# Attention with the values' product swapped, query heads turned whole, and an order of steps for each engine

## The chip, the core and the metric

The kernel runs on one core of a Trainium2 chip. The metric is the device time in microseconds (us) of one execution. The core has five engines with a queue each: TensorE (PE; its weight loads are shown apart as PEld), VectorE (DVE), ScalarE (ACT), GpSimd (POOL) and SyncE (SP), which here issues DMAs. They meet by semaphores only. SBUF is the working memory with 128 partitions, PSUM the banks that TensorE writes (8 banks of 128 partitions x 512 f32), DRAM the memory outside.

## What is computed

The input x is 8 sequences of 512 tokens with 256 channels. The reference adds to it a block "conditioning attention, then delta rule mixer", and then two mixtures of experts. Only the attention is touched here. Reduced to what matters:

```
q = norm(x) @ Wq            # 16 heads of 64
k, v = norm(x) @ Wkv        # one head of 64, shared by all query heads
s = 8 * l2norm(q) . l2norm(k) + relative bias, causal over key chunks, plus one null key
p = softmax(s)
o = p @ v   (null key: + p_null * v_null)
h = layernorm(o @ Wout)     # goes on to the delta phase, channels turned onto partitions
```

## The kernel before

Three phases follow one another: attention (`attention_phase`), the delta rule (`delta_phase`) and the mixtures. Between phases all engines meet.

**Tiles and heads.** The attention works on 32 query tiles of 128 tokens (`t`, 8 batches x 4). Tile i of a batch looks at i+1 key chunks of 128 keys; this number of chunks is w (1 to 4), and `width(n)` is 128 w. Each tile has 16 heads, numbered through as n = 16 t + h, 512 in all. One head is: scores (L455, two products of a 128-row operand that holds the high and the low part of the query, 64 rows each, with kT high and kT low); on VectorE the bias is added and the row minimum taken (L697); on ScalarE the exponential and its sum (L874); w transposes on TensorE (L465); their eviction from PSUM to PT, by VectorE for every fourth head (L708), else by ScalarE (L883); and the values' product (L478), for each key chunk one 128x128 f32 stationary operand PT with v as 64 moving columns. Its result stands with queries on partitions in the banks OB, 8 heads each. An f32 product is two records of the profile, a transpose or a product of fp32r is one. TensorE works with lags: in step n it does scores of head n, transposes of head n-2 (`QK_LAG`), the values' product of head n-4 (`PV_LAG`). GpSimd makes bias plus mask (L968) some heads ahead.

**Side steps.** Between the heads, each tile needs steps of its own. In front of its heads (`FRONT`, slots given against the tile before): statistics of x (stat, on DVE and POOL), xn, its turn xT, the projections q0, q1 and kv (L544), the sums of squares ss (POOL raises them to -0.5, L1001), qn, the turn of k (kT, L751 to L754), null, then the split of qn into high and low parts side by side in qs (qs0, qs1: cast on ACT L916, subtraction on POOL L1022), and the turns qT0 to qT3, four transposes each (L556), two copied out by ACT (L920) and two by DVE (L740). Behind its heads (`BACK`): diff and weigh per half of the heads, where the denominators become reciprocals rden and the null key's weights pnr, and the 8 heads of a bank are scaled into o (L616); oT, eight transposes (L569), copied out by ACT (L934) and DVE (L773); pnT, the turn of pnr (L575, L778); outp, the product with Wout plus the null key's part (L582, L583); statistics of the result, hn (L790), hT (L588, L940), and SP's store of it (L412).

**Order and banks.** `order()` merges heads and side steps into one list, which every engine walks; each does its own part of a step, in this order, and nothing overtakes. The side steps that need a PSUM bank share two, F0 and F1, as `FILLS` says. `fill` makes TensorE wait until the previous holder of the bank has been read, `filled` makes the reader wait for TensorE.

Of the kernel before, what the change touches and what calls it, by code (L numbers as in the profile page):

```python
# [6 lines left out]
F32 = mybir.dt.float32  # L7
# [5 lines left out]
P = 128  # L13
# [130 lines left out]
def attention_phase(nc, a, ident, delta, mixture, hT_out, bias_rows, hT_dram, inv_dram):  # L144


    QK_LAG, PV_LAG, S_SLOTS, PT_SLOTS = 2, 4, 5, 3
# [3 lines left out]
    with ExitStack() as ctx:  # L151
# [37 lines left out]
        qs = sb("qs", [P, NH, 2, DH], F32R)  # L189
# [7 lines left out]
        with ExitStack() as over:  # L197
            def mlp(name, shape):
# [26 lines left out]
        rden = sb("rden", [P, 2, NH // 2])  # L225
        pnr = sb("pnr", [P, P])
        pnrT = sb("pnrT", [P, P])
        o = sb("o", [P, NH, DH])
        stats2 = sb("stats2", [P, 6])
# [27 lines left out]
                 "q_high", "q_low", "kn_ready", "qT_act", "qT_dve", "kT_read", "kT_ready", "null_ready",  # L257
                 "scores_psum", "scores_ready", "probs_ready", "probsT_psum", "probsT_act", "probsT_dve", "pv_done",
                 "null_diff", "null_probs", "weights_ready", "o_scaled", "oT_act", "oT_dve", "pnrT_ready",
# [8 lines left out]
        mask_loaded = [sem(f"mask_loaded{i}") for i in range(2)]  # L268


        FRONT = {"stat": -5, "xn": -3, "xT": -2, "q0": 0, "q1": 1, "kv": 2, "ss": 3, "qn": 4, "kT": 7,
                 "null": 10, "qs0": 8, "qs1": 9, "qT0": 12, "qT1": 12, "qT2": 13, "qT3": 14}
        BACK = {"diff1": 0, "weigh1": 4, "oT": 6, "pnT": 7, "outp": 9, "hn": 11, "hT": 13}

        def order():
            behind = {}
            for t in range(NT + 1):
                if t < NT:
                    behind.setdefault(NH * t + 10, []).append(("diff0", t))
                    behind.setdefault(NH * t + 13, []).append(("weigh0", t))  # L280
                if t > 0:
                    for n, h in BACK.items():
                        behind.setdefault(NH * t + h, []).append((n, t - 1))
            for t in range(1, NT):
                for n, h in FRONT.items():
                    behind.setdefault(max(NH * (t - 1) + h, -1), []).append((n, t))
            behind.setdefault(6, []).append(("nullo", 0))
            for h in range(NH):
# [4 lines left out]
                     ("qs0", 0), ("qs1", 0), ("qT0", 0), ("qT1", 0), ("qT2", 0), ("qT3", 0),  # L293
                     ("narrow", 0)] + behind.get(-1, [])
            for n in range(NH * (NT + 1)):
                steps += [("head", n)] * (n < NH * NT + PV_LAG) + behind.get(n, [])
            return steps

        steps = order()
# [4 lines left out]
        for name, t in steps:  # L304
            for n in ([0, 1] if name == "oT" else [FILLS[name]] if name in FILLS else []):
                filling[name, t, n] = len(held[n]) + 1
                before[name, t, n] = held[n][-1] if held[n] else None
                held[n].append((name, t))

        def drained(name, t, n):  # L310
# [3 lines left out]
                    "qT0": [(s["qT_act"], 2 * t + 1)], "qT1": [(s["qT_dve"], 2 * t + 1)],  # L314
                    "qT2": [(s["qT_act"], 2 * t + 2)], "qT3": [(s["qT_dve"], 2 * t + 2)],
                    "kT": [(s["kT_read"], t + 1)], "oT": [((s["oT_act"], s["oT_dve"])[n], t + 1)],
# [3 lines left out]

        def evac_by_dve(n):
            return n % 4 == 3

        def count_dve(n):

            return (n + 1) // 4
# [28 lines left out]
        with nc.Block() as block:  # L355
            @block.sync
            def _(sp):
# [26 lines left out]
                for name, t in steps:  # L384
# [20 lines left out]
                    elif name == "head" and t % (NH * TT) == 0 and t // (NH * TT) + 2 < B:  # L405
                        b = t // (NH * TT)
                        sp.wait_ge(s["mask_read"], b + 1)
                        load_mask(b + 2)
# [13 lines left out]
            def _(pe):  # L422
# [16 lines left out]
                for name, t in steps:  # L439
                    if name == "head":  # L440
# [28 lines left out]
                        if 0 <= n < NH * NT:  # L469
# [5 lines left out]
                            if h == 8 and tile > 0:  # L475
                                pe.wait_ge(s["o_scaled"], 2 * tile)
# [2237 lines left out]
```

## Time and profile before

| | |
|---|---|
| time, median of 3 runs | 2559.46 us (2557.53 to 2559.73) |
| span of the profiled execution | 2563.2 us, mean granted clock 0.984 |
| first scores / last values' product of the attention | 55.0 / 1083.3 us |
| start of the delta phase | about 1099.6 us |
| TensorE busy | 2394.0 us, 93% of the span |
| VectorE / ScalarE / GpSimd busy | 1753.9 / 1234.0 / 1333.1 us |

The profile is one execution. No time of it is given beside the span; the span is 3.7 us above the median of the runs. A record of TensorE lasts from its start to its modelled end, and records overlap, so that the sum of durations is no time; what tells the pace is the distance of starts or of ends. Busy time counts overlapping records once.

### The profile page before, as it was taken

The page shows a single profiled execution, that of the slowest core. Times are in us where ns is not written, and L with a number is a line of the kernel's source. Part 1 is how long each engine was busy: PE and PEld are TensorE (multiplying, and loading weights), DVE is VectorE, ACT ScalarE, POOL GpSimd, SP SyncE. Part 2 cuts the span into 40 slices and gives each one's busy share as a digit, 9 for nine tenths or more (in the row PEclk, how much of TensorE's full clock was granted, in tenths as well). Part 3 has the DMA queues.
Part 4 walks back from the last instruction along what each step waited for, and adds up shares of the span by engine and source line. Part 5 has one row for each costly group of instructions (what it writes and reads, how often), then busy time and mean ns, then how long its engine had stood idle before and what let it go on. Part 6 is the DMA issues. An engine that isn't in the chain of part 4 may idle for free. (4 is left out here: it accounts for less than half of the span.)

```text
span 2563.2 us, 56453 instructions
## 1 busy us (share of the span) xinstructions
PE 2394.0 (93%) x20705; PEld 1977.5 (77%) x20705; DVE 1753.9 (68%) x4121; ACT 1234.0 (48%) x3133; POOL 1333.1 (52%) x1464
## 2 busy tenths in 40 slices
PE   5999999999999999977999999988899999999998
PEld 3788888888888888845777777766677877778776
DVE  4576767677767676677888888337865755746764
ACT  3656666666666666554555555114333333332332
POOL 3676767676767676535666666215422322322332
PEclk8999999999999999988999999999999999999999
DMA  4000100000000000001122221216022112111211
GB/s 143 7 11 9 46 18 11 10 10 9 11 10 9 10 5 5 5 15 24 40 56 55 55 53 47 55 59 181 32 66 63 55 58 67 58 47 62 66 34 59
DMA packets 156689, 105.05 MB, mean 41 GB/s; under 512 B 85168, under 2 KB 134832, under 8 KB 156416
## 3 DMA queue, kind: packets, MB, share of 16 engines
q1 hardware_dynamic: 130928, 62.69, 9.0%
q10 hardware_dynamic: 25488, 38.73, 4.9%
q8 instruction: 169, 2.77, 0.4%
q14 instruction: 104, 0.85, 0.1%
HBM read 80.51 MB, written 20.88 MB: 40 GB/s over the span
## 5 line engine op out<-in xcount | busy, mean ns | idle before, releaser
L968 POOL TENSOR_TENSOR a_bm<-a_bias,a_mask_add 128x512 f32<-128x512 f32 (+3 forms) x512 | 438.4, 873 | 189.3 <-DVE a_nm L697 186.3
L1592 POOL TENSOR_TENSOR m_hid_part<-m_hid,m_hid_part 128x512 fp32r<-128x512 f32 x176 | 238.5, 1355 | 552.9 <-ACT m_hid_part L1501 547.6
L874 ACT ACTIVATE a_S<-a_S,a_nm 128x512 f32<-128x512 f32 (+3 forms) x512 | 289.3, 565 | 347.6 <-DVE a_nm L697 344.9
L697 DVE CUSTOM_DVE_ANT_0 a_S<-a_S,a_bm,a_nsn 128x512 f32<-128x512 f32 (+3 forms) x512 | 275.3, 545 | 142.1 <-PE a_S L455 137.4
L478 PE MATMUL a_O<-a_v,a_PT 128*128 128x64 f32 x2560 | 342.4, 265 | 0.0
L478 PEld LDWEIGHTS a_O<-a_v,a_PT 128*128 128x128 f32 x2560 | 328.4, 193 | 0.0
L1513 ACT ACTIVATE m_hid<-m_G 128x512 f32<-128x512 f32 x176 | 105.4, 599 | 390.9 <-PE m_G L1447 353.3
L455 PE MATMUL a_S<-a_kT,a_qT 128*128 128x384 f32 (+3 forms) x1024 | 284.0, 358 | 3.6 <-DVE a_nm L697 3.2
L1674 DVE TENSOR_TENSOR m_hid<-m_hid,m_U 128x512 f32<-128x512 f32 x176 | 121.0, 687 | 223.8 <-PE m_U L1447 190.3
L1464 PE MATMUL m_Y<-m_hid_part,m_down_high 128*128 128x512 f32 x704 | 256.5, 405 | 12.2 <-POOL m_hid_part L1592 11.4
L1447 PE MATMUL m_G<-m_in,m_gate_high 128*128 128x512 f32 x704 | 252.2, 399 | 0.9 <-POOL m_up_low L1586 0.9
L1447 PE MATMUL m_U<-m_in,m_up_high 128*128 128x512 f32 x704 | 250.7, 396 | 1.5 <-DVE m_hid L1674 1.4
L465 PE MATMUL a_T<-s_ident,a_S 128*128 128x128 f32 x1280 | 227.0, 275 | 12.2 <-ACT a_PT L883 11.3
L465 PEld LDWEIGHTS a_T<-s_ident,a_S 128*128 128x128 f32 x1280 | 160.3, 140 | 42.2 <-ACT a_S L874 15.7
L455 PEld LDWEIGHTS a_S<-a_kT,a_qT 128*128 128x128 f32 x1024 | 163.8, 192 | 18.5 <-DVE a_nm L697 6.6
L1464 PEld LDWEIGHTS m_Y<-m_hid_part,m_down_high 128*128 128x128 f32 x704 | 132.8, 189 | 47.4 <-issue 18.0
L1447 PEld LDWEIGHTS m_U<-m_in,m_up_high 128*128 128x128 f32 x704 | 132.7, 188 | 35.0 <-DVE m_hid L1674 3.0
L1447 PEld LDWEIGHTS m_G<-m_in,m_gate_high 128*128 128x128 f32 x704 | 133.3, 189 | 33.9 <-POOL m_up_low L1586 1.4
L883 ACT COPY a_PT<-a_T 128x128 f32<-128x128 f32 (+3 forms) x384 | 156.2, 407 | 0.0
L1447 PE MATMUL m_G<-m_in,m_gate_low 128*128 128x512 f32 x352 | 140.6, 399 | 0.0
L1001 POOL TENSOR_TENSOR a_rr<-a_ss,a_half 128x17 f32<-128x17 f32 x32 | 98.5, 3077 | 79.8 <-DVE a_ss L736 79.8
L1464 PE MATMUL m_Y<-m_hid_part,m_down_low 128*128 128x512 f32 x352 | 139.4, 396 | 0.0
(323 smaller groups left out, 5348.4 us busy)
## 6 DMA issues: line engine op xcount, KB each, us to landing
m_spread<-s_w ACTq DMA_DIRECT2D x64, 256.0 KB, 3.2
m_spread<-s_w ACTq DMA_DIRECT2D x128, 128.0 KB, 2.9
a_x<-in_x SPq DMA_DIRECT2D x32, 128.0 KB, 2.2
s_hT<-a_hT SPq DMA_DIRECT2D x32, 128.0 KB, 2.1
d_x<-in_x SPq DMA_DIRECT2D x8, 512.0 KB, 4.7
d_h<-s_hT SPq DMA_DIRECT2D x8, 512.0 KB, 5.2
s_xg<-d_xg SPq DMA_DIRECT2D x8, 512.0 KB, 3.1
d_x<-s_xg SPq DMA_DIRECT2D x8, 512.0 KB, 4.6
```

What stands on the lines that cost most here:

```text
L455: last = pe.matmul(o_s[:, 0:w], qT[:, tile % 2, h], kT[tile // TT % 2][i][:, 0:w], start=i == 0, stop=i == 1)
L465: last = pe.transpose(TB[n % 2][:, j * P:(j + 1) * P], S[:, n % S_SLOTS, j * P:(j + 1) * P], ident[:])
L478: last = pe.matmul(OB[h // 8][:, (h % 8) * DH:(h % 8 + 1) * DH], PT[:, n % PT_SLOTS, j * P:(j + 1) * P], v[tile // TT % 2][:, j], start=j ...
L697: dve.tensor_tensor_reduce(S[:, n % S_SLOTS, 0:w], SB[n % 2][:, 0:w], bm[:, n % BM_SLOTS, 0:w], -1.0, nsn[:, tile % 2, h:h + 1], ALU.add, ...
L874: act.activation(S[:, n % S_SLOTS, 0:w], S[:, n % S_SLOTS, 0:w], ACT.Exp, scale=-1.0, bias=nm[:, tile % 2, h:h + 1], accum_out=den[:, tile ...
L883: act.copy(PT[:, n % PT_SLOTS, 0:w], TB[n % 2][:, 0:w]).then_inc(s["probsT_act"], 1)
L968: pool.tensor_tensor(bm[:, n % BM_SLOTS, 0:w], bias[:, h, L - w:L], mask_add[b % 2][:, 0:w], ALU.add).then_inc(s["bm_ready"], 1)
L1447: last = pe.matmul(dst[q % 2][:, :], wts[m][j][:, k, item], x[i][:, k], start=(i, j, k) == TERMS[0], stop=(i, j, k) == TERMS[-1])
L1464: last = pe.matmul(YB[k][:, :], down[m][j][:, item, k * P:(k + 1) * P], hid_part[i][:, q % H_SLOTS], start=item == 0 and i + j == 0, stop= ...
L1513: act.activation(hid[:, q % G_SLOTS], GB[q % 2][:, :], (ACT.Copy, ACT.Silu)[ITEMS[q][1]]).then_inc(gate_active, 1)
L1592: pool.tensor_tensor(hid_part[1][:, q % H_SLOTS], hid[:, q % G_SLOTS], hid_part[0][:, q % H_SLOTS].bitcast(F32), ALU.subtract).then_inc(hi ...
L1674: dve.tensor_tensor(h, h, UB[q % 2][:, :], ALU.mult).then_inc(mult_up, 1)
```

## The change

- The values' product works on two heads at once, after the second (odd) one. v is now the stationary operand, 128 rows by 64 columns, PT the moving one with 128 columns. The even head's result goes to partitions 0 to 63 of the bank, the odd one's to 64 to 127. So it comes out turned, channels on partitions, as the product with Wout wants it: the oT transposes and their copies go. PT has four slots instead of three.
- The reciprocals of the denominators stood one per partition and now must stand along the free axis, the same for 64 partitions. They are turned on TensorE (first half: new step wT0, 128x8; second half: in eight rows of pnT), copied to SBUF by VectorE, written to DRAM by SyncE and, once landed, read back to 64 partitions each with a zero stride, two transfers per half, 128 KB each. New steps scale0 and scale1 multiply the banks with them straight into oT.
- qn is turned whole, two heads per transpose, 8 per tile; the split follows. ScalarE copies one half of the partitions as the high part to its place, VectorE subtracts and writes the low part to the other half. qs and its two steps on ScalarE and GpSimd go.
- VectorE evicts one head of 16 (head 13) instead of four.
- One table SLOTS with offsets for each engine (LATER) takes the place of FRONT and BACK; each engine walks its own order. The banks F0 and F1 are dealt anew. The step outp is split into outp (TensorE) and ostat (statistics).

```diff
-    QK_LAG, PV_LAG, S_SLOTS, PT_SLOTS = 2, 4, 5, 3
+    QK_LAG, PV_LAG, S_SLOTS, PT_SLOTS = 2, 4, 5, 4
...
+        LATE = slice(2 * NH, 2 * NH + NH // 2)
+        weight = o[:].rearrange("p (i a) d -> p i (a d)", i=2)
...
+        SLOTS = {"stat": -21, "xn": -19, "xT": -18, "q0": -15, "q1": -15, "kv": -14, "ss": -13, "qn": -11, "kT": -9,
+                 "null": -7, "qT0": -8, "qT1": -7, "diff0": 7, "weigh0": 9, "wT0": 12, "diff1": 16, "scale0": 15,
+                 "weigh1": 14, "pnT": 19, "scale1": 24, "outp": 25, "ostat": 27, "hn": 28, "hT": 32}
+        LATER = {"PE": {}, "DVE": {"weigh1": 3, "ostat": -2, "scale0": 3, "weigh0": -1, "xT": 1, "pnT": 1, "qT1": 1,
+                 "diff1": -1, "hn": 1}, "ACT": {"hT": -1, "qT0": -1, "diff1": -1}, "POOL": {"qn": -1, "ostat": -1,
+                 "ss": 1}, "SP": {}}
...
+                behind.setdefault(max(NH * t + h + LATER[engine].get(n, 0), -1), []).append((n, t))
...
-        FILLS = {"xT": 0, "q0": 1, "q1": 0, "kv": 1, "qT0": 0, "qT1": 1, "qT2": 0, "qT3": 1, "kT": 0,
-                 "pnT": 1, "outp": 0, "hT": 1, "nullo": 0, "wide0": 0, "wide1": 1}
+        FILLS = {"xT": 1, "q0": 1, "q1": 0, "kv": 1, "qT0": 0, "qT1": 0, "kT": 0, "pnT": 0, "outp": 1, "hT": 0, "wT0":
+                 0, "nullo": 0, "wide0": 0, "wide1": 1}
...
+        DVE_HEADS = {13}
...
 sync:
+                    elif name in ("wT0", "pnT"):
+                        i = int(name == "pnT")
+                        sp.wait_ge(s["pnrT_ready" if i else "weightT_ready"], t + 1)
+                        sp.dma_start(weight_rows[i], pnrT[LATE, :] if i else weightT[:]).then_inc(weight_out, 16)
+                        sp.wait_ge(weight_out, 16 * (2 * t + 1 + i))
...
+                            sp.wait_ge(s["o_scaled"], 2 * t - 1 + i)
+                        for e in range(2):
+                            sp.dma_start(weight[e * DH:(e + 1) * DH, i].rearrange("p (a n) -> p a n", n=P),
+                                         bass.AP(tensor=weight_rows.tensor, offset=(i * NH // 2 + e) * P,
+                                                 ap=[[0, DH], [2 * P, NH // 4], [1, P]])).then_inc(weight_in[i], 16)
 tensor, head:
-                        if 0 <= n < NH * NT:
+                        if 0 <= n < NH * NT and n % 2 == 1:
...
-                                last = pe.matmul(OB[h // 8][:, (h % 8) * DH:(h % 8 + 1) * DH],
-                                                 PT[:, n % PT_SLOTS, j * P:(j + 1) * P], v[tile // TT % 2][:, j],
-                                                 start=j == 0, stop=j == tile % TT)
+                                for e in range(2):
+                                    last = pe.matmul(OB[h // 8][e * DH:(e + 1) * DH, at:at + P], v[tile // TT % 2][:, j],
+                                                     PT[:, (n - 1 + e) % PT_SLOTS, j * P:(j + 1) * P],
+                                                     start=j == 0, stop=j == tile % TT, skip_group_check=True)
...
-                            last = pe.transpose(f[:, j * P:(j + 1) * P],
-                                                qs[:, 4 * i + j].rearrange("p a d -> p (a d)").bitcast(F32), ident[:])
+                            last = pe.transpose(f[:, j * P:(j + 1) * P],
+                                                qn[:, 8 * i + 2 * j:8 * i + 2 * j + 2].rearrange("p a d -> p (a d)"), ident[:])
...
+                    elif name == "wT0":
+                        pe.transpose(f[0:NH // 2, 0:P], rden[:, 0], ident[:]).then_inc(full[FILLS[name]], 1)
 vector:
+                    to = pnr[:, LATE] if i else rden[:, 0]
+                    dve.reciprocal(to, dent[:, i]).then_inc(s["rden_ready"], 1)
...
+                def scale(t, i):
+                    dve.wait_ge(weight_in[i], 32 * (t + 1))
+                    dve.wait_ge(s["pv_done"], NH // 2 * t + 4 * (i + 1))
...
+                    dve.tensor_tensor(oT[:, 4 * i:4 * i + 4].rearrange("p a n -> p (a n)"), OB[i][:, :], weight[:, i],
+                                      ALU.mult).then_inc(s["o_scaled"], 1)
...
+                            dve.wait_ge(s["qT_high"], 4 * t + 2 * i + e + 1)
+                            dve.tensor_tensor(turned_heads(t, i, e)[other], heads_of(f)[own],
+                                              turned_heads(t, i, e)[own].bitcast(F32),
+                                              ALU.subtract).then_inc(s["qT_low"], 1)
 scalar:
-                        act.copy(qs[:, hs, 0], qn[:, hs]).then_inc(s["q_high"], 1)
+                        for e in range(2):
+                            act.copy(turned_heads(t, i, e)[halves(e)], heads_of(f)[halves(e)]).then_inc(s["qT_high"], 1)
 gpsimd:
-                        pool.tensor_tensor(qs[:, hs, 1], qn[:, hs], qs[:, hs, 0].bitcast(F32),
-                                           ALU.subtract).then_inc(s["q_low"], 1)
```

## Rows read from the trace of the kernel before

**Rows 1.** The page: busy time by engine, and the chain that ended last

```profile
PE 2394.0 (93%) x20705; PEld 1977.5 (77%) x20705; DVE 1753.9 (68%) x4121; ACT 1234.0 (48%) x3133; POOL 1333.1 (52%) x1464
...
PE 26%; DVE 2%; issue 2%; POOL 1%; ACT 0%; DMA 0%; ACTq 0%; SPq 0%; POOLq 0%; DVEq 0%
```

**Rows 2.** Busy time by stretch, four tiles of the third batch (w = 1, 2, 3, 4)

```profile
318.80:345.60 26.80, 24.30 (x178) 21.89 (x177) 16.65 (x65) 16.05 (x62) 17.13 (x24) 1.00 0.02 6
345.60:373.80 28.20, 25.77 (x185) 23.13 (x184) 20.93 (x66) 17.68 (x63) 21.41 (x25) 1.00 0.10 31
373.80:407.50 33.70, 31.75 (x236) 29.39 (x234) 25.35 (x66) 21.06 (x64) 26.19 (x25) 1.00 0.04 12
407.50:446.10 38.60, 38.34 (x283) 34.88 (x282) 27.82 (x68) 24.19 (x64) 26.01 (x26) 1.00 0.03 9
```

**Rows 3.** Groups by line and form, attention, TensorE: busy us, mean ns, idle before

```profile
L478 PE MATMUL a_O<-a_v,a_PT 128*128 128x64 f32 x2560 | 342.4, 265 | 0.0
```

**Rows 4.** Timeline of TensorE: start, length, records; w = 4, then the last heads

```profile
701.33 0.60 PE L465 MATMUL a_T<-s_ident,a_S 128*128 128x128 f32 x4
701.77 1.00 PE L478 MATMUL a_O<-a_v,a_PT 128*128 128x64 f32 x8
702.58 0.42 PE L455 MATMUL a_S<-a_kT,a_qT 128*128 128x128 f32 x2
...
1080.49 2.79 PE L478 MATMUL a_O<-a_v,a_PT 128*128 128x64 f32 x24
```

**Rows 5.** Timeline in the delta phase, then L2182 by record: min/median/max in ns

```profile
1299.67 0.41 PE L2235 MATMUL d_O<-d_S,d_qpT 64*32 64x64 f32 x8
1300.01 1.09 PE L2182 MATMUL d_R<-d_attn,d_uw 128*64 128x128 f32 x16
1301.04 0.44 PE L2092 MATMUL d_R<-s_ident,d_y 128*128 128x128 f32 x2
...
L2182 PEld LDWEIGHTS d_R<-d_attn,d_uw x256: 132/137/137, 1220.0 to 1685.9; 128*64 128x64 f32 x128
L2182 PE MATMUL d_R<-d_attn,d_uw x256: 272/273/323, 1220.0 to 1686.0; 128*64 128x128 f32 x128
```

**Rows 6.** Waits of TensorE, 60 to 1150 us: total us, times, longest

```profile
PE a_F L556 <- DVE a_hn L790: 11.6, 16, 0.9
...
PE a_F L556 <- ACT a_qT L920: 7.8, 24, 0.6
...
PE a_F L588 <- DVE a_qT L740: 5.2, 9, 1.0
PE a_F L575 <- DVE a_oT L773: 3.7, 8, 0.9
```

**Rows 7.** Groups by line and form on ACT, DVE and POOL, 60 to 1150 us

```profile
L883 ACT COPY a_PT<-a_T 128x512 f32<-128x512 f32 x96 | 54.2, 565 | 0.0
L916 ACT CAST a_qs<-a_qn 128x512 fp32r<-128x512 f32 x62 | 37.9, 611 | 0.0
L883 ACT COPY a_PT<-a_T 128x128 f32<-128x128 f32 x96 | 23.8, 247 | 0.0
...
L740 DVE CAST a_qT<-a_F 128x512 fp32r<-128x512 f32 x62 | 42.5, 685 | 8.8 <-PE a_F L556 8.7
L773 DVE COPY a_oT<-a_F 128x512 f32<-128x512 f32 x32 | 22.1, 691 | 24.1 <-PE a_F L569 24.1
...
L1022 POOL TENSOR_TENSOR a_qs<-a_qn,a_qs 128x512 fp32r<-128x512 f32 x62 | 78.9, 1272 | 3.8 <-ACT a_qs L916 3.8
```

**Rows 8.** DMA issues: KB each, median us to landing; page, then 60 to 1100 us

```profile
m_spread<-s_w ACTq DMA_DIRECT2D x128, 128.0 KB, 2.9
...
a_mask_in<-in_mask SPq DMA_DIRECT2D x5, 64.0 KB, 3.2
...
d_chunk_of<-in_c_chunk_of SPq DMA_DIRECT2D x1, 2.0 KB, 1.7
```

**Rows 9.** Timeline of TensorE at the end of the attention, in brackets idle time before

```profile
1086.92 5.33 PE L582 MATMUL a_F<-a_wout,a_oT 128*128 128x256 f32 x16 [0.59 <-DVE a_pnrT L778]
```

More of the change, by code:

```diff
@@ L188, in attention_phase @@
         kn = sb("kn", [P, 2, DH])
-        qs = sb("qs", [P, NH, 2, DH], F32R)
         qT = sb("qT", [P, 2, NH, P], F32R)
@@ L268, in attention_phase, with order @@
         mask_loaded = [sem(f"mask_loaded{i}") for i in range(2)]
[L271 to L275, printed above, removed]
-            behind = {}
[L277 to L286, printed above, removed]
+        weight_out = sem("weight_out")
+        weight_in = [sem(f"weight{i}_in") for i in range(2)]
+        SLOTS = {"stat": -21, "xn": -19, "xT": -18, "q0": -15, "q1": -15, "kv": -14, "ss": -13, "qn": -11, "kT": -9,
[4 more added lines that the diff above has]
+                 "ss": 1}, "SP": {}}
+        BACK = ("diff0", "weigh0", "wT0", "diff1", "scale0", "weigh1", "pnT", "scale1", "outp", "ostat", "hn", "hT")
+        def order(engine):
+            behind = {}
+            for t in range(NT):
+                for n, h in SLOTS.items():
+                    if t > 0 or n in BACK:
+                        behind.setdefault(max(NH * t + h + LATER[engine].get(n, 0), -1), []).append((n, t))
             behind.setdefault(6, []).append(("nullo", 0))
@@ L383, in _ @@
                 sp.dma_start(inv_dram.rearrange("s t h c i j -> (s t h c) (i j)"), null_flat).then_inc(s["inv_cleared"], 16)
-                for name, t in steps:
+                for name, t in order("SP"):
                     if name == "layer" and t == 1:
@@ L437, in fill @@
                     return FB[n]
-                for name, t in steps:
+                for name, t in order("PE"):
                     if name == "head":
@@ L546, in _ @@
                         last.then_inc(full[FILLS[name]], 1)
-                    elif name in ("qT0", "qT1", "qT2", "qT3"):
+                    elif name in ("qT0", "qT1"):
                         i = int(name[2])
@@ L768, in _ @@
                         weigh(t, int(name[5]))
-                    elif name == "oT":
-                        f = filled("oT", t, 1)
-                        if t > 0:
-                            dve.wait_ge(full[0], filling["outp", t - 1, 0])
-                        dve.tensor_copy(oT[:, 4:8].rearrange("p a n -> p (a n)"), f[:, :]).then_inc(s["oT_dve"], 1)
+                    elif name == "wT0":
+                        f = filled(name, t)
+                        dve.tensor_copy(weightT[:], f[0:NH // 2, 0:P]).then_inc(s["weightT_ready"], 1)
+                    elif name in ("scale0", "scale1"):
+                        scale(t, int(name[5]))
                     elif name == "pnT":
@@ L823, in _ @@
                                   a["L0_cond_Wkv"][k * P:(k + 1) * P, :]).then_inc(w_loaded[k], 16)
-                for name, t in steps:
+                for name, t in order("ACT"):
                     if name == "gain":
@@ L929, in _ @@
                         act.activation(pn[:, i], dn[:, i], ACT.Exp).then_inc(s["null_probs"], 1)
-                    elif name == "oT":
-                        f = filled("oT", t, 0)
-                        if t > 0:
-                            act.wait_ge(full[0], filling["outp", t - 1, 0])
-                        act.copy(oT[:, 0:4].rearrange("p a n -> p (a n)"), f[:, :]).then_inc(s["oT_act"], 1)
                     elif name == "hT":
@@ L974, in _ @@
                 link(pool.memset(pnr[:], 0.0))
-                for name, t in steps:
+                for name, t in order("POOL"):
                     if name == "head":
@@ L1003, in _ @@
                         pool.wait_ge(s["rr_ready"], t + 1)
+                        if t > 0:
+                            pool.wait_ge(full[FILLS["qT1"]], filling["qT1", t - 1])
                         pool.wait_ge(s["q_ready"], 2 * (t + 1))
```

163 lines of the change are left out of this document (75 added, 88 removed).

## The prediction, made before the changed kernel ran

> **What bounds the kernel now.** I first read the page for the engine shares and the slices. TensorE is busy 2394.0 of 2563.2 us; the chain that ended last reaches back only into the mixtures, 26% of the span on TensorE and 2% on the next [rows 1]. The attention, which alone is changed, ends at 1096 us, its heads run from 55 to 1083. So the second view is the busy time by stretch over one batch of four query tiles, one of eight alike [rows 2]. The reader is to see that TensorE idles 0.26 us in the widest tile (38.34 of 38.60), 1.95 in the next, 2.4 and 2.5 in the two narrow ones. VectorE has 10.8, 8.3, 7.3 and 10.1 us left in them, ScalarE more. So TensorE's own work is the bound in the wide tiles, and in the narrow ones a chain of small waits between engines. Third come the groups of TensorE: the values' product (L478) is the costliest, 342.4 us [rows 3]. Fourth, its timeline, since a mean of pipelined records doesn't tell their pace. Last, the waits [rows 6], for what the new order can remove.
>
> **Values' product: from 128x64 moving to two 64-column tiles.** In the widest tile the transposes end at 701.33+0.60 = 701.93, the 8 records of one head at 701.77+1.00 = 702.77, and the next scores at 703.00 [rows 4]. So 8 records take 0.84 us from end to end, near 0.112 each, the first 0.06 (24 in a row take 2.79 us [rows 4], 0.109 each without the last one's latency). With w key chunks a head takes 0.17, 0.40, 0.62, 0.84 us for w = 1 to 4, and a pair of heads twice that.
> After, a pair of heads has 4w records again, but two by two in the column halves of the array. No row of the attention shows that. The delta phase has the same form, 128 rows x 64 columns with 128 moving, alternating halves as here: 16 records in 1.09 us [rows 5]; less one record's latency of 0.273, 15 steps of 0.054, so two records per 0.109. The price is a change of the array's shape at both sides. Into that form: the records before end at 1300.08, the 16 at 1301.10, 1.02 us where 8 steps of 0.109 are 0.87, so 0.15 extra. Out of it: two transposes end 0.38 us later where 0.22 is usual, so 0.16 extra. A pair of heads then takes 0.218w + 0.31 = 0.53, 0.75, 0.96, 1.18 us, against 0.34, 0.80, 1.24, 1.68: +0.19, -0.05, -0.28, -0.50. There are 8 batches x 8 pairs of each width: 64 x (-0.64) = **-41 us**. Bounds: the switches can't cost less than nothing (-120), and at 0.45 us instead of 0.31 the sum is -5. I take the measured 0.31, as that form is the same.
>
> **Transposes.** A full 128x128 one costs 0.11 us ((0.60-0.27)/3 [rows 4]). The turn of query heads whole takes 8 instead of 16 of them per tile, and the 8 of the output go (L569). One small one (128x8) is new. 32 x (16 x 0.109 - 0.11) = **-52 us**. Together -93: -10 in a tile with four chunks, hardly anything in one with a single chunk beyond the transposes' 1.6.
>
> **The other engines.** ScalarE loses two casts of 0.611 and the 512-wide copy to oT per tile, gains two 512-wide copies (four half-height ones for two full ones) and 3 of 16 more evictions, 0.247 to 0.565 each: +0.1 to +1.1 us. VectorE loses two casts of 0.685, the copy of 0.691 and three evictions, at most as long, gains four subtractions of half height from PSUM (I take 0.69, as the 512-wide cast from PSUM; 0.35 if height counts, 1.0 if the crossing of halves does) and the small copy of the turned weights, under 0.3: +0.1 to -1.1. The scaling stays one product per half. GpSimd loses two of 1.272 [rows 7]. All this fits beside TensorE: in the widest tile VectorE would have 26.7 us of 32 to do, ScalarE 25.3. What is close is not the sum but where they block.
>
> **Waits that go.** The new turn stands on a bank whose holder before was kT, not outp; oT, which filled both banks, is gone. The four waits that hang on this are 11.6, 7.8, 5.2 and 3.7 us [rows 6]: **-28 us** (0 to -40, the latter as small waits hide in the latency of records that count as busy).
>
> **Waits that come.** (1) qT1 fills the bank that qT0 filled one head before; it is free after two copies on ScalarE and two subtractions on VectorE, some 0.59+3x0.69 = 2.7 us after the transposes, while one head of a narrow tile lasts under 1.2 us on TensorE. (2) The reciprocals now travel: turned, written to DRAM, read back to 64 partitions each by two transfers, all on SyncE. A small transfer lands in 1.7 us; a broadcast of 64 KB took 3.2, one of 128 KB 2.9 [rows 8]. With 0.6 us for the issue between: 1.7+0.6+3.2 = 5.5 to 6. For the first half this lies between slots 12 and 18 and is hidden. For the second, VectorE copies pnrT at slot 20 and waits in scale1 at slot 24 of the next tile, four heads: some 2.7, 4.2, 5 and over 6 us by that tile's width (an estimate: per head 0.34 us of scores and one transpose at w = 1 [rows 4], a pair of products every second head, and above that ScalarE, which has some 0.7 to 1.2 us for each head). So it is late by 3, 1.5, 0.8 and 0. Behind scale1 stand VectorE's next heads and its subtractions for qT0, thus qT1 and outp on TensorE; two heads of slack absorb a part, and (1) falls together with it. I take 5.5 us per batch for both: **+44 us**. Bounds: 0 if the trip takes 4 us and ScalarE has its copies done; at 8 us it is 5.3+3.8+3+2 = 14 per batch, 112.
> SyncE's queue holds x loads, masks and hT's store beside these; at the points passed none waits for anything later than the transfers do, so nothing there is added.
>
> **The two ends.** At the end nothing hides the trip: before, the last product ends at 1083.3 and outp starts at 1086.92 [rows 9]. After, pnT no longer waits for the product, its trip of 5.5 to 6 us starts near 1082.5 on that scale, then 0.7 for the scaling: outp at 1089.5, **+3**. In front of the first head qT1's wait for the bank costs 2.7 us and the two split steps that go give back 0.6 + 1.3 [rows 7]: **+1**.
>
> **Sum.** -93 - 28 + 44 + 4 = -73 us. The profiled execution has a span of 2563.2, 3.7 above the median 2559.46 of the runs; in runs: **2486 us**.
>
> **A rule against this.** The record rows say loads run beside the matmuls in flight: 16 loads of up to 0.137 us lie within the 1.09 us of the 16 records [rows 5]. The Trainium skill, page "TensorE: Matmul & The Clock Gate", section "Part 3: Packing small matmuls — row/col tiling", says that a weight load overlaps with matmuls in flight only where the row group differs, and two column halves share their rows. By that rule, each of the 1280 record pairs would show its load; as a mechanism of this kernel that is 1280 x 0.137 = +175 us, 2661 in all. The trace disagrees with it at the same form.
>
> **Rivals.**
> A. *The new waits are hidden.* The trip takes near 4 us or the lead of two heads takes it up. Then -93-28+4, 2442 us. For: VectorE has 7 to 10 us left per tile [rows 2]. Against: those are exactly the narrow tiles where TensorE already waits though nobody is full.
> B. *The trip is long.* 8 us, as SyncE's two broadcasts have small pieces (512 bytes) and come one behind the other: -93-28+112+4 = -5, so 2554; about 2545 where slack absorbs some. For: broadcasts are the slowest small transfers of rows 8. Against: the queues are near empty in the attention, a DMA share of 0.02 to 0.10 [rows 2].
> C. *The halves don't run side by side*, since here each record adds to the sum of the one before last in the same bank. Then a pair of heads costs 0.218w more, mean 0.545, x 256 = +140: 2626, **slower than before**. Place: L478's successor; it decides from where about half of the overlap is lost. It is also the case in which the change doesn't do what it says. Against: 0.054 per record in rows 5, though there every product stands alone.
> D. The exposed loads above, 2661.
>
> **Chances.** My forecast 0.46, A 0.25, B 0.22, C 0.05, D 0.02. Beside the forecast's own 2465 to 2507, the range goes 2430 to 2542: it leaves out C and D, about 0.1 of B and little of A. A measurement of this kernel tells 0.2% (5 us) from no change; faster by more: 0.46 + 0.25 + most of B = 0.90; within: 0.02; slower: 0.08 (C, D and the end of B).
>
> **What would show it.** The product's group has 2560 records of 128*64 with 128 moving, two starting within a few ns, and its busy time falls to 200 us or less; a pair of heads ends 1.18 us behind its transposes at w = 4 and 0.53 at w = 1 (wrong: 2.0 and 0.75, rival C). The widest tile lasts 33 us instead of 38.6, the narrowest stays near 26. Waits: TensorE's on qT's low half and VectorE's on the weights' DMA, longest behind slot 24 in the narrow tiles; if the DMA's is under 1 us, A; over 3 in wide tiles too, B. From the last product to outp some 6 us instead of 3.6. All behind the attention keeps its length; if it doesn't, the forecast is wrong for a reason not named here.

## The result, and the profile after

The changed kernel takes 2532.3 us (median of 4 runs, 2526.3 to 2541.4), the kernel before 2559.6 on the same chip. The ratio is 0.9889, 95% interval 0.9859 to 0.9918: 27 us faster. The forecast was 73 us faster. Direction and range held, the size was less than half of the forecast.

The page of the changed kernel (busy time, share of the span, instructions; the granted TensorE clock in 40 slices of the span; then two groups of its list), beside [rows 1, 3]:

```profile
PE 2324.1 (92%) x20225; PEld 1800.3 (71%) x20225; DVE 1751.1 (69%) x4089; ACT 1257.3 (50%) x3197; POOL 1259.7 (50%) x1400
...
PEclk8998989899999999898999999999999999999999
...
L492 PE MATMUL a_T<-s_ident,a_S 128*128 128x128 f32 x1280 | 234.7, 281 | 35.7 <-ACT a_PT L914 32.8
L508 PE MATMUL a_O<-a_PT,a_v 128*64 128x128 f32 x2560 | 202.8, 289 | 0.4 <-ACT a_PT L914 0.4
```

The values' product falls from 342.4 to 202.8 us, as forecast (200 or less). TensorE as a whole loses only 69.9 us of busy time, where 93 us of work went. The clock's row has 8s among the first ten slices; the same row of the kernel before is

```profile
PEclk8999999999999999988999999999999999999999
```

The busy time by stretch, the third batch again, tiles with one to four key chunks, beside [rows 2] (length, then busy time of TensorE, of its weight loads, of VectorE, ScalarE, GpSimd; granted clock, DMA share, GB/s):

```profile
308.30:337.70 29.40, 26.11 (x163) 20.10 (x161) 17.97 (x67) 16.71 (x66) 14.47 (x21) 0.83 0.07 21
337.70:366.00 28.30, 25.31 (x171) 19.30 (x169) 19.78 (x65) 18.11 (x64) 18.18 (x22) 0.94 0.16 47
366.00:396.10 30.10, 28.35 (x222) 22.55 (x218) 24.30 (x67) 21.83 (x66) 23.78 (x23) 1.00 0.12 34
396.10:431.10 35.00, 33.19 (x267) 26.21 (x265) 28.04 (x67) 25.33 (x66) 24.98 (x26) 1.00 0.10 30
```

Before, these four took 26.8, 28.2, 33.7 and 38.6 us, all at a clock of 1.00. The wide tiles gained 3.6 us each. The narrowest got 2.6 us longer, and its TensorE is busy 1.8 us more, though it has less to do: its clock is 0.83.

Where that comes from stands in the timeline of TensorE in that tile (start, length, records; in brackets the idle time before and what ended it):

```profile
317.19 0.44 PE L508 MATMUL a_O<-a_PT,a_v 128*64 128x128 f32 x4
317.78 0.44 PE L482 MATMUL a_S<-a_kT,a_qT 128*128 128x128 f32 x2
318.55 0.30 PE L492 MATMUL a_T<-s_ident,a_S 128*128 128x128 f32 x1 [0.33 <-ACT a_PT L914]
...
321.08 0.47 PE L590 MATMUL a_F<-s_ident,a_kn 128*128 128x128 f32 x1 [1.32 <-POOL a_kn L1028]
321.21 0.67 PE L482 MATMUL a_S<-a_kT,a_qT 128*128 128x128 f32 x2
...
323.68 0.70 PE L508 MATMUL a_O<-a_PT,a_v 128*64 128x128 f32 x4
324.52 5.27 PE L604 MATMUL a_F<-a_wout,a_oT 128*128 128x256 f32 x16
...
330.42 0.42 PE L482 MATMUL a_S<-a_kT,a_qT 128*128 128x128 f32 x2
```

The same four records of the product take 0.44 us at 317.19 and 0.70 at 323.68; the same two of the scores 0.44, 0.67, and 0.42 again from 330.42. In between the clock records show half of the full 2.4 GHz, that is 1.2. Before it fell TensorE had had single transposes and pairs of records between short waits, last one of 1.32 us. Summed over the 31 tiles behind the first, TensorE is at the lower level (1.2 GHz) for 88.8 us; before, for none.

The waits of TensorE from 60 to 1080 us (total, times, longest), beside [rows 6]:

```profile
PE a_T L492 <- ACT a_PT L914: 32.8, 75, 0.7
PE a_F L604 <- DVE a_oT L645: 24.6, 24, 6.0
PE a_F L590 <- POOL a_kn L1028: 9.2, 7, 1.3
...
PE a_F L558 <- DVE a_xn L748: 4.8, 6, 1.0
...
PE a_F L610 <- DVE a_hn L822: 2.1, 1, 2.1
```

The four waits that were to go are gone. The 2.1 us on hn stand at the very end, as they do in the trace of before; new are 2.1 us of query heads' turns on GpSimd's qn and 1.2 us of wT0 on qT. In the trace of before, from 60 to 1080 us, the wait of a transpose for ScalarE's copy was

```profile
PE a_T L465 <- ACT a_PT L883: 11.3, 30, 0.5
```

and is 32.8 now; outp's for the scaled output (24.6, of which 6.0 at the very end) and kT's for kn are new or larger.

**The ledger.** From the records of both profiled runs, TensorE, in us, what changed against before:

| part | forecast | measured |
|---|---|---|
| tiles 2 to 32, TensorE busy (930.4 to 867.5) | -93 | -62.9 |
| tiles 2 to 32, TensorE idle (56.6 to 80.5) | -28 + 44 = +16 | +23.9 |
| first tile (35.6 to 38.3) | +1 | +2.7 |
| last scores to the delta phase (21.9 to 25.1) | +3 | +3.2 |
| in front of the first head, and all behind the attention | 0 | +0.3 - 5.9 |
| span (2563.2 to 2524.5) | -73 | -38.7 |

The profiled run of the changed kernel is the fastest of its four, hence 38.7 here and 27 in the medians. A second profile of it has the same middle (948.7 us for tiles 2 to 32 against 948.0) and a span of 2534.1; of the 9.6 us between the two spans 7.2 lie behind the attention, which the change doesn't touch, and 2.7 in the first tile. The row to explain is the first: 30 us of busy time.

### The profile page after: what moved, and what is told of

It is laid out like the page before. It is cut to its first block and busy times, and to the rows that moved or that the text cites. A ratio compares the mean times of both kernels' runs of the same rounds, so it can differ in the third digit from the quotient of the medians.

```text
span 2524.5 us, 55790 instructions
## 1 busy us (share of the span) xinstructions
PE 2324.1 (92%) x20225; PEld 1800.3 (71%) x20225; DVE 1751.1 (69%) x4089; ACT 1257.3 (50%) x3197; POOL 1259.7 (50%) x1400
## 5 line engine op out<-in xcount | busy, mean ns | idle before, releaser
L482 PE MATMUL a_S<-a_kT,a_qT 128*128 128x384 f32 (+3 forms) x1024 | 294.4, 372 | 4.5 <-DVE a_nm L725 1.9
L1475 PE MATMUL m_Y<-m_hid_part,m_down_high 128*128 128x512 f32 x704 | 256.5, 405 | 12.3 <-POOL m_hid_part L1603 11.5
L492 PE MATMUL a_T<-s_ident,a_S 128*128 128x128 f32 x1280 | 234.7, 281 | 35.7 <-ACT a_PT L914 32.8
L508 PE MATMUL a_O<-a_PT,a_v 128*64 128x128 f32 x2560 | 202.8, 289 | 0.4 <-ACT a_PT L914 0.4
L482 PEld LDWEIGHTS a_S<-a_kT,a_qT 128*128 128x128 f32 x1024 | 170.3, 204 | 42.7 <-DVE a_nm L725 20.5
L914 ACT COPY a_PT<-a_T 128x128 f32<-128x128 f32 (+3 forms) x480 | 198.8, 414 | 1.4
L508 PEld LDWEIGHTS a_O<-a_PT,a_v 128*64 128x64 f32 x2560 | 137.0, 139 | 43.3 <-issue 36.3
L604 PE MATMUL a_F<-a_wout,a_oT 128*128 128x256 f32 x512 | 131.8, 415 | 25.3 <-DVE a_oT L645 24.6
```

What stands on the lines that cost most here:

```text
L482: last = pe.matmul(o_s[:, 0:w], qT[:, tile % 2, h], kT[tile // TT % 2][i][:, 0:w], start=i == 0, stop=i == 1)
L492: last = pe.transpose(TB[n % 2][:, j * P:(j + 1) * P], S[:, n % S_SLOTS, j * P:(j + 1) * P], ident[:])
L508: last = pe.matmul(OB[h // 8][e * DH:(e + 1) * DH, at:at + P], v[tile // TT % 2][:, j], PT[:, (n - 1 + e) % PT_SLOTS, j * P:(j + 1) * P], ...
L604: pe.matmul(f[:, 0:D], oT[:, i], wout[:, i], start=i == 0, stop=False)
L914: act.copy(PT[:, n % PT_SLOTS, 0:w], TB[n % 2][:, 0:w]).then_inc(s["probsT_act"], 1)
L1475: last = pe.matmul(YB[k][:, :], down[m][j][:, item, k * P:(k + 1) * P], hid_part[i][:, q % H_SLOTS], start=item == 0 and i + j == 0, stop= ...
```

## The experiments

Theory 1, after the traces: the clock. With less work in the narrow tiles TensorE is granted 1.2 GHz for a part of them, and what it then does costs more. Rival 2: the trip of the reciprocals through DRAM, which the forecast had priced, together with rival 4's wait, at 44 us. Rival 3: ScalarE, which took three evictions per tile from VectorE and whose copies now hold TensorE 32.8 us. Rival 4: the bank that qT1 shares with qT0.

**The changed kernel again**, as it is, beside the first four:

> The changed kernel once more, on the chip of the experiments, as the base of their comparison. Both theories: 2526 to 2541 us as before, TensorE at half clock for about 13 us in each batch, in the tile with one chunk and at the start of the next, and nowhere else among the heads.

2534.6 us (2532.9 to 2539.8), ratio 0.9893 [0.9875, 0.9911]. Same as the result.

**Products that nobody reads, in the narrowest tiles (theory 1).**

```
+ def keep_busy(n, h):
+     words = ident[:].bitcast(BF16)
+     for _ in range(n):
+         pe.matmul(OB[0 if h <= 10 else 1][:, 3 * P:], words[:, 0:P], words[:, 0:P], start=True, stop=True, ...)
  for name, t in order("PE"):
+     if name == "kT" and (t - 1) % TT == 0 and t > 1:
+         keep_busy(16, 7)
...
+                 if tile % TT == 0 and tile > 0 and h >= 6:
+                     keep_busy(4, h)
```

> Adds work that nobody reads: in the tiles with one key chunk (but the first), 16 bf16 products of 128 columns before kT, where TensorE waits 1.3 us for GpSimd, and 4 behind the scores of heads 6 to 15; 56 per tile, 3.1 us at full clock. Clock theory (the changed kernel leaves TensorE so little work in the narrow tiles that it is given half the clock there, and then pays it in outp and the projections): the half-clock stretches among the heads go, the narrow tile falls from 29.4 to 27.5 us and the next from 28.3 to 27, 20 to 30 us in all, 2505. Rival (the narrow tile is held by its chain through GpSimd and ScalarE, and the clock only follows): clock at full, time within 5 us of the changed kernel or up to 15 us above it.

2515.9 us, ratio 0.9807 [0.9783, 0.9830]: 19 us faster than the changed kernel, with more work on TensorE. The narrowest tile falls from 29.4 to 27.4 us (mean of seven batches). 30.7 us at the lower level remain in tiles 2 to 32, 22.8 of them in the eight two-chunk tiles.

**The same in the tiles with two chunks too.**

```
-                 if tile % TT == 0 and tile > 0 and h >= 6:
+                 if tile % TT < 2 and tile > 0 and h >= 6:
```

> As the kernel with unread products in the one-chunk tiles, and 4 of them behind the scores of heads 6 to 15 in the two-chunk tiles too (2.2 us each at full clock). That kernel (2516) still had 3.3 us at half clock in each two-chunk tile. If those come from that tile's own small load, they go and the time stays or falls to 2508; if they come from what the tile before did, they stay and the time rises by 5 to 15 us for the added work.

2506.8 us, ratio 0.9783 [0.9767, 0.9798]: 28 us faster than the changed kernel, the fastest kernel of this study, 2.2% below the kernel before. Its stretches of the third batch:

```profile
307.31:334.23 26.92, 25.14 (x220) 20.22 (x218) 17.50 (x67) 16.48 (x65) 13.99 (x21) 1.00 0.07 21
334.23:361.25 27.02, 25.53 (x212) 20.19 (x210) 20.82 (x67) 18.57 (x65) 19.00 (x22) 1.00 0.19 52
```

29.40 and 28.30 us are 26.92 and 27.02, at a clock of 1.00, with 98 records more. The lower level among tiles 2 to 32 is 3.4 us instead of 88.8. TensorE's waits from 60 to 1080 us:

```profile
PE a_F L615 <- DVE a_oT L656: 25.9, 31, 5.8
PE a_T L503 <- ACT a_PT L925: 16.4, 46, 0.7
PE a_F L601 <- POOL a_kn L1039: 5.6, 15, 0.4
```

**The same products in the kernel before**, which has no lower level there to lose: the control.

> The kernel before with the same unread products as in the best run so far (16 before kT of the one-chunk tiles' successors, 4 behind the scores of heads 6 to 15 in tiles with one and two chunks). Clock theory: there is no half clock among its heads to give back, so the work only costs: 2562 to 2585. Rival (the unread products help by shifting TensorE's steps against the other engines): faster than 2560 here too.

2578.1 us, ratio 1.0058 [1.0042, 1.0075]: 16 us slower. The products are no gain by themselves in that kernel (by what they delay or how they space the engines). In tiles 2 to 32 they add 32.8 us of busy time there (930.4 to 963.1) and 12.3 us of length. In the changed kernel the same products add 0.5 us of busy time (867.5 to 868.0) and take 22.9 us of length away (948.0 to 925.1). The difference of the busy times, 32 us, is what the lower level had cost TensorE: the 30 us that the ledger misses. In length the difference is 35 us, if the products' own price is the same in both kernels. That the products fill waits is not the difference: idle time falls by 20.4 us in the kernel before (56.6 to 36.2) and by 23.3 in the changed one (80.5 to 57.2).

The control also shows what the products do to a wait with no clock in play. The wait of the transposes for ScalarE's copies was 11.3 us before and is here

```profile
PE a_T L476 <- ACT a_PT L894: 1.9, 8, 0.2
```

**Fewer of them**, two for four per head:

```
-                 keep_busy(4, h)
+                 keep_busy(2, h)
```

> As the best run so far (2507), with 2 unread products instead of 4 behind each of those heads' scores (1.1 us less work per tile at full clock). If what it takes is only that TensorE has something to do, the clock stays full and the time is 2500 to 2507; if half-clock stretches come back in the two-chunk tiles, 2512 to 2520.

2514.8 us, ratio 0.9815 [0.9801, 0.9830]. A part of the lower level is back, 41.0 us from the first head to the last against 10.2, and 8 us with it: less work and a longer time. The 16 products in the gap before kT are still there, so it is not that gap alone that lowers the clock.

**And in the first tile**:

```
-                 if tile % TT < 2 and tile > 0 and h >= 6:
+                 if tile % TT < 2 and h >= 6:
```

> As the best run so far (2507), with the 4 unread products behind the scores of heads 6 to 15 in the very first tile too. The first tile lasts 38 to 41 us against 34 to 36 before the change, with a half-clock stretch behind it: if the clock is its cause, 2 to 4 us less, 2503; if it is the new steps' chain, nothing changes, 2505 to 2510.

2511.8 us, ratio 0.9794 [0.9777, 0.9811], no gain. The first tile takes 40.1 us against 39.8, with 3.4 us at the lower level instead of 6.8: what the clock returns there the added products take.

**The trip left out (rival 2).** The reciprocals make their DMAs for the first tile only; later tiles are scaled by that tile's.

```
- elif name in ("wT0", "pnT"):
+ elif name in ("wT0", "pnT") and t == 0:
...
- dve.wait_ge(weight_in[i], 32 * (t + 1))
+ dve.wait_ge(weight_in[i], 32)
```

> Leaves out the transfers of the reciprocals for all tiles but the first, so that they are scaled with stale weights; the turns and copies stay. As the prediction has it (the trip is late by 3, 1.5, 0.8 us in the narrow tiles): 40 us less and the end 4 us earlier, 2488. Rival, from the changed kernel's waits (VectorE waits 6.1 us in all for these transfers, 4.9 of them in the last tile): only 4 to 7 us less, 2527.

2522.6 us, ratio 0.9844 [0.9825, 0.9863]: 12 us faster than the changed kernel. Tiles 2 to 32 take 948.5 us against 948.7 on the same chip: the trip costs nothing there. Most of the gain lies behind the last head, where the last scores to the delta phase are 17.8 us against 25.6; 1.3 us lie in the first tile and the rest outside the attention. The two ends, the changed kernel's first:

```profile
1045.78 1.09 PE L508 MATMUL a_O<-a_PT,a_v 128*64 128x128 f32 x16 [0.40 <-ACT a_PT L914]
1047.49 0.27 SPq L426 DMA_DIRECT2D s_weight_rows<-a_pnrT  x1
1048.90 1.24 SPq L434 DMA_DIRECT2D a_o<-s_weight_rows  x2
1052.35 0.69 DVE L645 TENSOR_TENSOR a_oT<-a_O,a_o 128x512 f32<-128x512 f32 x1 [4.88 <-DMA a_o<-s_weight_rows]
...
1053.09 6.20 PE L604 MATMUL a_F<-a_wout,a_oT 128*128 128x256 f32 x16 [5.96 <-DVE a_oT L645]
```

Without the trip:

```profile
1046.68 1.09 PE L508 MATMUL a_O<-a_PT,a_v 128*64 128x128 f32 x16 [0.41 <-ACT a_PT L914]
1048.28 0.68 DVE L645 TENSOR_TENSOR a_oT<-a_O,a_o 128x512 f32<-128x512 f32 x1
...
1049.02 3.72 PE L604 MATMUL a_F<-a_wout,a_oT 128*128 128x256 f32 x16 [0.98 <-DVE a_oT L645]
```

From the write's issue to the scaling the trip takes 1052.35 - 1047.49 = 4.9 us. And it costs twice: after the 6 us of idle time the 16 products take 6.20 us, most of it at the lower level (1051.3 to 1058.2), instead of 3.72 us.

**The second half scaled one head earlier**, in the kernel with the products in both narrow tiles. What hid the trip in the middle?

```
- LATER = {... "DVE": {"weigh1": 3, "ostat": -2, ...
+ LATER = {... "DVE": {"weigh1": 3, "scale1": -1, "ostat": -2, ...
```

> The changed kernel with the unread products in one- and two-chunk tiles (2507) and VectorE's scale1 one head earlier, since TensorE waits 25.9 us in 31 tiles for it in front of outp and VectorE waits only 6.1 us for its transfer. If the transfer has slack there: 5 to 12 us less, 2498. If the trip of 4.9 us is then late, VectorE waits in the narrow tiles, as the prediction feared at slot 24: 2510 to 2530.

2576.8 us, ratio 1.0064 [1.0041, 1.0087]: 70 us slower than the same kernel with the scaling at its place. VectorE's waits from 60 to 1080 us, then TensorE's:

```profile
DVE a_oT L656 <- DMA a_o<-s_weight_rows: 83.7, 31, 5.0
```

```profile
PE a_F L595 <- DVE a_kf L794: 64.6, 30, 4.6
```

That is 2.7 us of VectorE's wait in each of 31 tiles, from one head. TensorE stays busy 27 us longer too and is at the lower level for 68.3 us instead of 3.4, so the 70 us are this wait and what the clock adds to it. At its own place the scaling stands on VectorE behind the subtraction of kT, which waits for kn and TensorE (34.8 us in all in the changed kernel), and by then the data are there: from 60 to 1040 us VectorE waits 1.3 us for them. One head earlier it comes in front of that subtraction. The trip was the danger that the forecast saw; the order hides it by one step.

**Evictions back to VectorE (rival 3)**, four per tile instead of one:

```
- DVE_HEADS = {13}
+ DVE_HEADS = {3, 7, 11, 15}
```

> VectorE evicts heads 3, 7, 11, 15 again instead of 13 alone; all else as changed. Theory that ScalarE's evictions hold TensorE (33 us of waits of the transposes on ScalarE's copies): those waits fall by half and the kernel is 10 to 15 us faster, 2520. Rival (VectorE is as late as ScalarE in the wide tiles): waits move to scores and oT, 2535 to 2550.

2552.0 us, ratio 0.9963 [0.9949, 0.9976]: 17 us slower than the changed kernel. TensorE's wait for ScalarE's copies stays (32.8 to 34.3), and one for VectorE comes (4.8 to 18.5):

```profile
PE a_T L492 <- ACT a_PT L914: 34.3, 76, 0.7
...
PE a_F L558 <- DVE a_xn L748: 18.5, 21, 2.0
```

With two per tile in the kernel with the products:

```
- DVE_HEADS = {13}
+ DVE_HEADS = {5, 13}
```

> As the best run so far (2507), VectorE evicts heads 5 and 13 instead of 13 alone. If TensorE's 16 us of waits for ScalarE's copies are ScalarE's load, they halve: 2500. If VectorE is by now as near its limit (back to four evictions cost 17 us), 2510 to 2515.

2509.1 us, ratio 0.9780 [0.9766, 0.9795] against 0.9783: no difference, and the wait for ScalarE's copies is 16.4 us with and without. Rival 3 falls: the load of ScalarE isn't what those waits hang on.

**The bank between qT0 and qT1 (rival 4).** outp stands between them on TensorE. Here it comes one step later, so that qT1 is in front of it.

```
- LATER = {"PE": {}, "DVE": {"weigh1": 3, "ostat": -2, ...}, "POOL": {"qn": -1, "ostat": -1, ...
+ LATER = {"PE": {"outp": 1}, "DVE": {"weigh1": 3, "ostat": -1, ...}, "POOL": {"qn": -1, ...
```

> The changed kernel with outp one head later on TensorE (and its statistics one later on VectorE and GpSimd): TensorE waits 18.7 us in 23 tiles for VectorE's scale1 in front of outp. If that wait is lost time, 10 to 18 us less, 2520; if TensorE then waits at the next place instead (the transposes for ScalarE's copies), within 4 us of 2535.

2661.9 us, ratio 1.0390 [1.0370, 1.0410]: 127 us slower than the changed kernel.

```profile
PE a_F L584 <- DVE a_qT L771: 99.4, 28, 4.8
```

The wait for qT0's split, which the forecast feared, is 3.6 us in each of 28 tiles here; in the changed kernel it shows once, 2.3 us, before the first head. There 3.7 us of output products stand in front of qT1 and cover it (the 16 records at 324.52 in the timeline above are the same step at half clock).

**One order for all engines**, the steps where most of them stand:

```
- LATER = {"PE": {}, "DVE": {"weigh1": 3, "ostat": -2, "scale0": 3, ...}, "ACT": {...}, "POOL": {...}, "SP": {}}
+ LATER = {e: {"weigh1": 3, "ostat": -2, "scale0": 3, "weigh0": -1, "diff1": -1, "pnT": 1} for e in (...)}
```

> The changed kernel with one order for all engines: the same slots, and VectorE's offsets of weigh, scale0, diff1, pnT and ostat for every engine; the other offsets of LATER go. If an order of their own is worth much, 10 to 25 us slower than the changed kernel (2535), 2545 to 2560; if the engines' waits are set by the sums and chains and not by these offsets, within 5 us.

2584.1 us, ratio 1.0078 [1.0059, 1.0096]: 49 us slower than the changed kernel, with this one common order; whether another one would do better was not tried.

```profile
PE a_F L589 <- POOL a_kn L1027: 43.7, 29, 2.0
PE a_S L481 <- DVE a_nm L724: 35.9, 30, 1.6
```

**The turn alone, in the kernel before** (query heads whole, split behind the turn; the values' product, the order and the eviction of before):

```
- "qs0": 8, "qs1": 9, "qT0": 12, "qT1": 12, "qT2": 13, "qT3": 14
+ "qT0": 12, "qT1": 13
...
+ act.copy(turned_heads(t, i, e)[halves(e)], heads_of(f)[halves(e)])
+ dve.tensor_tensor(turned_heads(t, i, e)[other], heads_of(f)[own], turned_heads(t, i, e)[own].bitcast(F32), ALU.subtract)
```

> The kernel before with one part of the change alone: query heads turned whole (8 transposes per tile instead of 16) and split behind the turn; qT0 at slot 12, qT1 at 13. The forecast's step (each transpose gone is 0.109 us saved on TensorE, wherever it stands): 28 us less, 2532. Clock theory: only the tiles with 3 and 4 chunks give it, 14 us, and in the narrow tiles nothing is gained or half-clock stretches appear: 2545 to 2560.

2737.9 us, ratio 1.0688 [1.0669, 1.0708]: 176 us slower than before, though it takes eight transposes, two casts of ScalarE and two subtractions of GpSimd out of each tile. TensorE's waits, then VectorE's:

```profile
PE a_F L560 <- ACT a_hT L940: 110.8, 26, 4.7
```

```profile
DVE a_qT L747 <- ACT a_qT L921: 73.4, 53, 1.9
```

With the halves at other slots and on the other banks (qT0 at slot 8, qT1 at 12):

> The kernel before with the whole turn of query heads alone, as in the run that was 176 us slower, but with the banks dealt so that no one stands behind the split: qT0 on bank 1 at slot 8 (behind pnT), qT1 on bank 0 at slot 12 (behind outp, as qT0 stood). If that run's loss was the wait of hT's and qT1's bank (106 us of waits and 256 us at half clock), it goes: 2535 to 2550, the wide tiles 0.9 us shorter each. If the split behind the turn is itself too long for ScalarE and VectorE, it stays above 2600.

2682.6 us, ratio 1.0474 [1.0452, 1.0497]: still 121 us slower.

```profile
PE a_F L534 <- DVE a_xn L724: 100.5, 27, 4.2
```

```profile
DVE a_qT L747 <- ACT a_qT L921: 88.7, 56, 1.9
```

The blocked step of TensorE changes with the slots, VectorE's wait in front of the subtraction stays: 1.4 us a time, then 1.6. Each subtraction needs ScalarE's copy of the same bank, so in one order for all engines VectorE stands still while ScalarE reaches it, and what is behind it (xn, the heads) is late. In the changed kernel, where ScalarE's copies of qT0 come one head earlier and VectorE's subtractions of qT1 one later, the same wait is, from 60 to 1080 us,

```profile
DVE a_qT L771 <- ACT a_qT L944: 0.2, 1, 0.2
```

## Why the prediction was right or wrong

**The values' product: right.** At four chunks the changed kernel's timeline has

```profile
406.67 0.60 PE L492 MATMUL a_T<-s_ident,a_S 128*128 128x128 f32 x4
407.20 1.09 PE L508 MATMUL a_O<-a_PT,a_v 128*64 128x128 f32 x16
408.23 0.73 PE L482 MATMUL a_S<-a_kT,a_qT 128*128 128x512 f32 x2
```

From the end of the transposes (407.27) to the end of the product (408.29) 1.02 us, where 0.87 + 0.15 was forecast; the next scores, with 512 columns, end 0.67 us later (408.96). By the records that median is 0.66 us (25 times) and was 0.52 before (42 times): 0.14 more. With the 128-column scores of [rows 4] it is 0.37 against 0.23, 0.14 again. For one to four chunks the records give 0.37, 0.59, 0.81 and 1.02 us, and 0.14 on top: 0.51, 0.73, 0.95, 1.17 against the forecast's 0.53, 0.75, 0.96, 1.18. Rivals C (2.0 at four chunks) and D fall. The loads of this group are 139 ns each and lie beside the records, as the form in [rows 5] had it; the rule weighed against it does not hold for this form here.

**All of TensorE's work, -93: right at full clock, by an estimate.** Without the unread products' 32.8 us (from the control) the busy time of the kernel with them would be 868.0 - 32.8 = 835.2, 95 us less than before.

**The step that failed** is not in the sum at all, a cost put at nothing: the forecast took TensorE's records at the durations of before, at a clock of 1.00 in every stretch of [rows 2], and left them there. The change takes busy time out of tiles in which TensorE idled 2.5 us already (some 1.8 us in the narrowest, an estimate by the control) and puts new waits into them. TensorE now has gaps there, is granted 1.2 GHz for 88.8 us of tiles 2 to 32, and gives back 30 of 93 us. That this is the clock and not the gaps is shown by the pair of runs with unread products: 28 us gained where the lower level is, 16 lost where there is none. In length the clock took 35 us of tiles 2 to 32, by the same pair. Without it they would be 39 + 35 = 74 us shorter (an estimate), where -93 + 16 = -77 was forecast: the clock is nearly the whole miss there. Not separated is what in the change lowers it, the work taken out or the new 1.3 us waits for kn: the unread products filled both.

**"Narrowest stays near 26": wrong, by the clock.** It lasts 29.4 us. With the clock back at 1.00 it is 26.9 us in the third batch, with 56 unread products in it. In the control these products make the same tile 1.0 us longer (26.80 to 27.79), so some 25.9 us would be left (an estimate). The forecast's own terms took next to nothing out of this tile: 8 x 0.19 us more for the products, 1.6 us less for the transposes. What sets its length beside TensorE, which idles 1.8 of the 26.9 us, is not shown by a run. A part of the chain in front of kT is GpSimd's; in the changed kernel it reads

```profile
317.47 3.08 POOL L1019 TENSOR_TENSOR a_rr<-a_ss,a_half 128x17 f32<-128x17 f32 x1 [1.31 <-DVE a_ss L764]
320.63 0.40 POOL L1028 TENSOR_TENSOR a_kn<-a_qraw,a_rr 128x128 f32<-128x128 f32 x1
```

and kT's transpose starts at 321.08.

**"The widest tile lasts 33 us": it lasts 35.0, at full clock.** Its busy time falls by 5.2 us, where 5.6 was forecast (8 x 0.50 + 1.6; the "-10 in a tile with four chunks" is a slip). But it now idles 1.8 us instead of 0.3: 0.9 for ScalarE's copies and 0.9 for the scaled output. So TensorE's work alone no longer sets the length there.

**Waits that go, -28: named right, worth little.** All four of [rows 6] went. The time came back as others (32.8 on ScalarE's copies, 24.6 on the scaled output, 9.2 on kn).

**Waits that come, +44: both wrong in the middle.** The bank was priced by the length of the split, without what stands between on TensorE: outp, 3.7 us. With outp one step later the wait is there, 99.4 us. The trip's length was 4.9 us, below the 5.5 to 6 I took and above the 4 of rival A; what hid it was one step in VectorE's order, not its length. Rival A's mechanism (waits hidden) so took place, but its sum took the -28 in full and knew no clock. Rival B falls. Taken together, idle time rose 24 us where +16 was forecast: close by number and by luck, with none of its terms right.

**The own order of each engine was priced at nothing.** It is worth 49 us against the one common order that was tried, and turning the heads whole in the common order of before costs 121 and 176 us at the two placements tried. So the gain hangs on that part of the change.

**The ends.** Product to outp 6.2 us (1046.87 to 1053.09), 6 forecast; +3.2 us against +3, a part of it by the clock (outp takes 6.20 us, and 5.33 before [rows 9]). The first tile is 2.7 us longer in the profile of the ledger, 4 to 5.4 in most others, where +1 was forecast. Its idle time rises 2.5 us in it (5.6 to 8.1), and that is the forecast's own wait for the bank, now on the bias's turn; the first of TensorE's waits from 55 to 94 us is

```profile
PE a_F L552 <- DVE a_qT L771: 4.0, 2, 2.3
```

I had taken 2.7 us for it and set 1.9 us of steps that go against it; those gave nothing back. What is above 2.7 us in the other profiles goes with the clock: the second profile of the changed kernel has 10.2 us at the lower level in this tile, this one 3.4, at the same idle time.

**Open.** Which step ahead of ScalarE's copies makes the transposes wait 32.8 us: not its load, as the two runs with other evictions show. With the unread products it is 16.4 us, but that is not the clock's share: in the control the same products cut this wait from 11.3 to 1.9 us at full clock. How each wait divides between the chain and the clock is worked out by differences of two kernels, not measured by itself.

## What to carry to other kernels

Read the granted clock as part of the cost: taking work from TensorE in stretches where it already waits, or adding waits there, can lower it, and then the work that is left gets dearer. Where the profile after shows that, products that nobody reads, put in those gaps, can pay for themselves; in a stretch at full clock they only cost. Price a new wait by what stands between the two instructions on the waiting engine, in each engine's own order, and mind that one step can be worth 70 us: 2.7 us of exposed wait in each of 31 tiles, and the clock's part on top. An engine that must wait for another one's copy of the same bank needs its step later than the other's, not beside it: VectorE's wait for ScalarE's copies was 0.2 us that way, against 73 and 89 in a common order.

## What the hardware showed that was not expected

A wait cost nearly half as much again through the clock. With one order for all engines the idle time of tiles 2 to 32 rises 42 us and the busy time another 18, with outp one step later 92 and 43, at the same work; the time at the lower level rises from 88.8 to 130 and 229 us. Half the partitions saved next to nothing. VectorE's subtraction from PSUM over 64 partitions and 512 columns takes 689 ns, its scaling product from PSUM over 128 partitions 684. ScalarE's cast from PSUM over 64 partitions takes 579 ns, and 590 over 128 in the kernel before:

```profile
L771 DVE TENSOR_TENSOR a_qT<-a_F,a_qT 64x512 fp32r<-64x512 f32 x128 | 88.2, 689 | 9.0 <-ACT a_qT L944 5.1
L645 DVE TENSOR_TENSOR a_oT<-a_O,a_o 128x512 f32<-128x512 f32 x64 | 43.8, 684 | 6.2 <-DMA a_o<-s_weight_rows 6.1
L944 ACT CAST a_qT<-a_F 64x512 fp32r<-64x512 f32 x128 | 74.2, 579 | 90.4 <-PE a_F L584 88.8
```
